# Perceiver block on one core: context columns of two tiles loaded transposed, tail groups of 80 rows, scans spread

## What is computed

```python
energy = jnp.einsum('bcn,bmn->bcm', x1, x2)            # x1: layernormed x (16,64,1024), x2: context (16,1601,1024)
attn = jax.nn.softmax(energy, axis=-1)
attn = attn / (RENORM_EPS + attn.sum(axis=1, keepdims=True))
x_r = jnp.einsum('bcm,bmn->bcn', attn, x1_2)           # x1_2: the same context
t = x1 - (jnp.einsum('oc,bcn->bon', conv_w, x_r) + conv_b[None, :, None])
t_hat = (t - mean) * jax.lax.rsqrt(var + BN_EPS)       # mean and var over batch and width
x_r_out = jax.nn.relu(t_hat * bn_gamma[None, :, None] + bn_beta[None, :, None])
return x1 + x_r_out
```

## Time and profile before

| | |
|---|---|
| median of 3 runs | 1380.77 us (1377.85 to 1381.84) |
| the profiled execution | 1379.24 us, its span 1377.4 us |
| TensorE busy (matmuls) | 1334.1 us, 97% |
| VectorE, ScalarE busy | 878.7 us (64%), 495.1 us (36%) |
| DMA | 356.25 MB, mean 259 GB/s; 379 to 422 GB/s in the first 13 of 40 slices |

### The profile page before, as it was taken

One profiled execution on the slowest core, in us unless ns is written; L12 is line 12 of the kernel. 1 busy time (PEld: TensorE's weight loads), 2 busy tenths in 40 slices (PEclk: granted clock), 3 DMA queues, 4 the chain that ended last, 5 costly groups with the idle time before them and its releaser, 6 DMA issues.

```text
span 1377.4 us, 17833 instructions
## 1 busy us (share of the span) xinstructions
PE 1334.1 (97%) x6850; PEld 651.2 (47%) x6850; DVE 878.7 (64%) x1484; ACT 495.1 (36%) x765; POOL 2.4 (0%) x10
## 2 busy tenths in 40 slices
PE   7999999999999979999999999999999999999994
PEld 4554646444454434444555555444444444444442
DVE  3232424324242288888889996755999997777974
ACT  1121302113021122116877775112545455544432
POOL 0000000000000000000000000000000000000000
PEclk9999999999999989999999999999999999999998
DMA  9999999999999587845565669341487775222264
GB/s 379 419 421 420 421 422 420 422 421 421 417 398 393 234 321 255 315 168 164 161 182 154 172 174 339 107 168 52 167 271 226 242 264 196 77 77 77 77 180 152
DMA packets 141044, 356.25 MB, mean 259 GB/s; under 512 B 63008, under 2 KB 89760, under 8 KB 115360
## 3 DMA queue, kind: packets, MB, share of 16 engines
q1 hardware_dynamic: 137792, 343.56, 68.5%
q10 hardware_dynamic: 3168, 11.54, 2.1%
HBM read 308.40 MB, written 46.66 MB: 258 GB/s over the span
## 4 chain that ended last, share of the span: by engine, by line
PE 74%; issue 14%; DMA 6%; DVE 4%; ACT 1%; DVEq 0%; POOLq 0%; POOL 0%
PE ps L1048 13%; PE ps L1153 13%; PE ps L1309 9%; PE ps L1220 8%; PE ps L962 7%; PE ps L1269 6%; PE ps L1107 5%; PE ps L1000 4%; DMA ctxT<-in_ctxT 3%; PE ps L979 2%; PE ps L1030 2%; PE ps L982 2%; DMA w_scan<-in_w2t 1%; PE ps L1173 1%; DMA x_t<-in_x 1%
## 5 line engine op out<-in xcount | busy, mean ns | idle before, releaser
L1358 PE MATMUL ps<-t_half,hl 128*128 128x512 f16 x896 | 193.6, 379 | 0.0
L1048 PE MATMUL ps<-ctx_sb,attnT 128*64 128x512 f32 (+1 forms) x832 | 180.3, 593 | 0.0
L699 ACT ACTIVATE stg<-ps 128x512 f32<-128x512 f32 (+1 forms) x80 | 44.4, 555 | 345.5 <-PE ps L979 173.4
L1358 PEld LDWEIGHTS ps<-t_half,hl 128*128 128x128 f16 x896 | 87.7, 98 | 105.7
L962 PE MATMUL ps<-ctxT,x1T 128*64 128x512 f32 x512 | 115.8, 596 | 1.8 <-DMA ctxT<-in_ctxT 1.8
L872 ACT ACTIVATE hl<-hb,al 128x512 f16<-128x512 f32 x112 | 79.2, 720 | 97.4 <-PE ps L1358 83.7
L1048 PEld LDWEIGHTS ps<-ctx_sb,attnT 128*64 128x64 f32 (+1 forms) x832 | 58.9, 137 | 115.4 <-issue 108.0
L1862 DVE SCALAR_TENSOR_TENSOR hl<-hb,al,hl 128x512 f16<-128x512 f32 x112 | 81.9, 749 | 48.7 <-ACT hl L872 48.5
L1107 PE MATMUL ps<-wv_sb,x2T 128*128 128x512 f32 x256 | 112.0, 596 | 0.0
L1220 PE MATMUL ps<-wo_sb,oT 128*128 128x512 f32 x256 | 111.6, 593 | 0.3 <-ACT oT L778 0.3
L1456 DVE COPY stg<-ps 128x512 f32<-128x512 f32 (+1 forms) x80 | 50.9, 639 | 82.2 <-PE ps L982 43.0
(11 more groups left out here) (220 smaller groups left out, 1810.5 us busy)
## 6 DMA issues: line engine op xcount, KB each, us to landing
ctxT<-in_ctxT SPq DMA_DIRECT2D x64, 1024.0 KB, 22.4
ctx_sb<-in_ctx SPq DMA_DIRECT2D x40, 1024.0 KB, 17.3
ctx_sb<-in_ctx SPq DMA_DIRECT2D x8, 4096.0 KB, 28.3
ctx_sb<-in_ctx SPq DMA_DIRECT2D x16, 2048.0 KB, 32.5
w_scan<-in_w1t SPq DMA_DIRECT2D x32, 512.0 KB, 6.4
w_buf<-in_w1t SPq DMA_DIRECT2D x32, 512.0 KB, 4.1
w_scan<-in_w2t SPq DMA_DIRECT2D x32, 512.0 KB, 5.5
w_buf<-in_w2t SPq DMA_DIRECT2D x32, 512.0 KB, 4.7
```

The costliest lines, as they stand in the source:

```text
L1048: ins = mm(bank(ea + hf)[C * b:C * b + C, :], attnT[0:w, slots[mt], C * b:C * b + C], ctx_sb[0:w, mt, b, hf * BANK:hf * BANK + BANK], star ...
L1358: ins = mm(bank(b), hl[:, r % RING, n, s * P:s * P + P], t_half[:, r % BRING, :], start=(fresh and k == 0 and n == 0), stop=(k == HK - 1 a ...
```

## The change

It has five parts.

1. For tile 6 the wide columns (positions 1024 to 1535) of all eight 128s of the width come transposed from memory: `in_ctxW`, four loads of 1 MiB through the ring `ctxT` behind the tile's eight chunks. TensorE multiplies them directly (`loaded_energies`), and only the two tail pairs are transposed.
2. For tile 7 the wide columns come so too, two loads through the ring and two "apart" into `stg`, and the tail columns as `in_ctxE`, two loads of 0.25 MiB into `tails`. The apart and tail loads have one semaphore, and TensorE waits for all four ahead of the third wide load. Tile 7 has no transposes of context at all.
3. The row group of block 12 is loaded as 80 rows (0.625 MiB) for 128, in all eight tiles.
4. SP's order for tiles 6 and 7 is another (below), and `tok` and `xo` are loaded as two row tiles each at first and the rest behind `wv_sb`.
5. VectorE's first part has 40 scans for 48, placed before, within and behind the row tiles' work (`V_SCANS`); the second part has 24 for 16, four per row tile.

With this `make_x1` of tile 7 is called behind the copy of the first tail pair and the maximum over the chunk energies, and the relu of row tile 2 behind ScalarE's copies for row tile 0.

```diff
@@ -41,6 +41,7 @@
+TAIL_ROWS = TAIL + (-TAIL) % 16
...
@@ -56,16 +57,40 @@
-PAIRS = [("wide", c) for c in range(NC)] + SINGLES[-2:]
-E = len(PAIRS)
-assert len(SINGLES) == E
+LOADED = (0,) * (NT - 2) + (8, NC)
+def pairs(p):
+    if p < BY_ROW:
+        return SINGLES
+    return [("wide", c) for c in range(LOADED[p], NC)] + (SINGLES[-2:] if p < NT - 1 else [])
+def first_pair(p):
+    return sum(len(pairs(q)) for q in range(p))
+def slots_of_tile(p):
+    ring = [(p, "chunk", c) for c in range(NC)] + [(p, "wide", i) for i in range(LOADED[p] // 2 if p < NT - 1 else 2)]
+    return ring if p < NT - 1 else ring + [(p, "apart", i) for i in range(2)]
+USES = [use for p in range(NT) for use in slots_of_tile(p)]
+USE_NO = {use: n for n, use in enumerate(USES)}
+RING_NO = {use: n for n, use in enumerate([use for use in USES if use[1] != "apart"])}
+RING_USES = list(RING_NO)
-SCANS_V = 48
+SCANS_V = 40
+V_SCANS = (0, 0, 2, 6, 7, 7, 7, 7, 4)
...
@@ -143,6 +168,7 @@
+        tails = [sb("tail0", [P, NC // 2, 2, TAIL], 168 * KB), sb("tail1", [P, NC // 2, 2, TAIL], 180 * KB)]
...
@@ -405,15 +443,28 @@
             sp.dma_start(x_t[:, :], x_v[0]).then_inc(x_in, 16)
             sp.dma_start(cst[:, :], consts).then_inc(cst_in, 16)
-            def load_T(q, chunks):
+            def load_T(q, chunks, kind="chunk"):
                 for c in chunks:
-                    k = NC * q + c
+                    use = (q, kind, c)
+                    k = RING_NO[use]
                     if k >= SLOTS:
-                        sp.wait_ge(ctxT_used, k - SLOTS + 1)
-                    sp.dma_start(ctxT[:, k % SLOTS, :, :], ctxT_in[q, c]).then_inc(ctxT_got[k % SLOTS], 16)
+                        sp.wait_ge(ctxT_used, USE_NO[RING_USES[k - SLOTS]] + 1)
+                    to, src = (slot(use), ctxT_in[q, c]) if kind == "chunk" else (halves(use), ctxW_in[q, c])
+                    sp.dma_start(to, src).then_inc(ctxT_got[k % SLOTS], 16)
+
+            def load_apart():
+
+                sp.wait_ge(e_done, first_pair(NT - 1))
+                for i in range(2):
+                    sp.dma_start(slot((NT - 1, "apart", i)), ctxW_in[NT - 1, 2 + i]).then_inc(apart_got, 16)
+                for i in range(2):
+                    sp.dma_start(tails[i][:, :, :, :], ctxE_in[i]).then_inc(apart_got, 16)
             def load_N(q, g):
                 m0, m1 = N_GROUPS[g][0], N_GROUPS[g][-1] + 1
+                if m1 == MT:
+                    sp.dma_start(ctx_sb[0:TAIL_ROWS, m0, :, :], ctx[q, m0 * P:m0 * P + TAIL_ROWS]).then_inc(ctx_in[g], 16)
+                    return
                 sp.dma_start(ctx_sb[:, m0:m1, :, :], ctx[q, m0 * P:m1 * P].rearrange("(t p) b n -> p t b n", p=P))\
                   .then_inc(ctx_in[g], 16)
...
@@ -445,28 +496,49 @@
                     next_N(range(1, 5))
                 else:
                     load_T(p + 1, range(7, NC))
+                    load_T(p + 1, range(min(LOADED[p + 1] // 2, 2)), "wide")
+                    if p + 1 == NT - 2:
+                        next_N((4, 0))
+                        load_T(p + 1, range(2, 4), "wide")
+                        next_N((1,))
+                        load_T(p + 2, range(0, 2))
+                        next_N((2, 3))
+                        load_T(p + 2, range(2, 4))
+                        next_N(range(5, G))
+                        load_T(p + 2, range(4, 6))
+                        continue
+                    if p + 1 == NT - 1:
+                        load_apart()
+                        next_N((5, 7, 0, 1, 2, 6, 3, 4))
+                        break
                     next_N(range(0, 5))
                 if p == 0:
                     sp.dma_start(lam_sb[:, 0:4 * D], lambdas.partition_broadcast(P)).then_inc(lam_in, 16)
                 if p + 2 < NT:
-                    load_T(p + 2, range(0, 4 if p < 2 else 2))
+                    load_T(p + 2, range(0, 4 if p < 2 or LOADED[p + 1] else 2))
                 next_N(range(5, 6))
-                if p >= 2 and p + 2 < NT:
+                if p >= 2 and p + 2 < NT and not LOADED[p + 1]:
                     load_T(p + 2, range(2, 4))
                 next_N(range(6, G))
                 if p + 2 < NT:
                     load_T(p + 2, range(4, 6))
-            sp.wait_ge(ctxT_used, NC * NT)
+            def load_tok(t0, t1):
+                sp.dma_start(tok[:, t0:t1, :], n_dram[t0:t1].rearrange("t p n -> p t n")).then_inc(n_in, 16)
+
+            def load_xo(t0, t1, s):
+                sp.dma_start(xo[:, t0:t1, :], x_v[t0:t1].rearrange("t p n -> p t n")).then_inc(s, 16)
+
+            sp.wait_ge(ctxT_used, len(USES))
             sp.wait_ge(n_stored, 16 * (NT - 1))
-            sp.dma_start(tok[:, 0:NT - 1, :], n_dram[0:NT - 1].rearrange("t p n -> p t n")).then_inc(n_in, 16)
+            load_tok(0, 2)
             sp.wait_ge(pv_done, G * NT - 7)
-            for i in range(2):
-                h4 = slice(4 * i, 4 * i + 4)
-                sp.dma_start(xo[:, h4, :], x_v[h4].rearrange("t p n -> p t n")).then_inc(s_in[i], 16)
+            load_xo(0, 2, s_in[0])
             sp.wait_ge(pv_done, G * NT - 3)
             sp.dma_start(wv_sb[:, :, :], wv.rearrange("(c p) n -> p c n", p=P)).then_inc(wv_in, 16)
+            load_tok(2, NT - 1)
+            load_xo(2, NT, s_in[1])
             sp.wait_ge(pv_done, G * NT)
             def scan_load(n, buf):
...
@@ -739,6 +811,9 @@
+                if t == 0:
+                    act.wait_ge(n_in, 32)
+                    relu(2)
...
@@ -1001,17 +1076,41 @@
+            def loaded_energies(p):
+                wides = [u for u in slots_of_tile(p) if u[1] != "chunk"]
+                for j, use in enumerate(wides):
+                    if use[1] == "apart":
+                        pe.wait_ge(apart_got, 64)
+                    else:
+                        k = RING_NO[use]
+                        pe.wait_ge(ctxT_got[k % SLOTS], 16 * (k // SLOTS) + 16)
+                    for i in range(2):
+                        c = 2 * j + i
+                        for b in range(2):
+                            ins = mm(bank(2)[C * b:C * b + C, :], x1T[:, p % 2, c, C * b:C * b + C], halves(use)[:, i, b, :],
+                                     start=(c == 0), stop=(c == NC - 1))
+                    ins.then_inc(ctxT_used, 1)
+            def tail_energies(p):
+                for c in range(NC):
+                    for b in range(2):
+                        ins = mm(bank(3, TAIL)[C * b:C * b + C, :], x1T[:, p % 2, c, C * b:C * b + C],
+                                 tails[c // 4][:, c % 4, b, :], start=(c == 0), stop=(c == NC - 1))
+                ins.then_inc(e_done, 1)
-                for e in range(4, E, 2):
+                n = len(pairs(p))
+                for e in range(4, n, 2):
-                two(pair_energies, p, E - 2)
+                two(pair_energies, p, n - 2)
...
@@ -1073,7 +1172,16 @@
-                if p + 1 < NT:
+                if p + 1 < NT and LOADED[p + 1]:
+                    chunk_energies(p + 1, range(4, NC))
+                    if p == 5:
+                        loaded_energies(6)
+                        two(pair_transposes, 6, 0)
+                        later_pairs(6)
+                    else:
+                        loaded_energies(7)
+                        tail_energies(7)
+                elif p + 1 < NT:
...
@@ -1435,8 +1543,8 @@
-                if t % 4 == 0:
-                    V.wait_ge(s_in[t // 4], 16)
+                if t in (0, 2):
+                    V.wait_ge(s_in[t // 2], 16)
@@ -1450,20 +1558,25 @@
-                    if E * p + e >= 4:
-                        V.wait_ge(e_done, E * p + e - 3)
+                    if first_pair(p) + e >= 4:
+                        V.wait_ge(e_done, first_pair(p) + e - 3)
-                    if e == 7:
-                        V.wait_ge(ctxT_used, NC * (p + 1))
+                    if e == max(len(pairs(p)) - 3, 0):
+                        V.wait_ge(ctxT_used, used_by(p))
-                    if e == 5 and p + 1 < NT:
+                    if e == max(len(pairs(p)) - 5, 0) and p + 1 < NT:
-                V.wait_ge(e_done, E * p + E - 2)
+                if p < NT - 1:
+                    V.wait_ge(e_done, first_pair(p + 1) - 2)
+                else:
+                    V.wait_ge(ctxT_used, used_by(p))
+                    own.done(V.tensor_reduce(mx4[:, 0:1], ps[:, ea * BANK:(ea + 2) * BANK], AX.X, ALU.max))
+                    V.wait_ge(ctxT_used, len(USES))
-                V.wait_ge(e_done, E * p + E)
+                V.wait_ge(e_done, first_pair(p + 1) if p < NT - 1 else first_pair(p) + 1)
...
@@ -1528,11 +1643,20 @@
-            def norm2(t):
+            def next_scans(n):
+                for _ in range(n):
+                    scan(scanned_tiles[0], w_scan)
+                    scanned_tiles[0] += 1
+                    if scanned_tiles[0] == WT:
+                        V.wait_ge(scanned, WT)
```

(48 more changed lines are left out.)

25 lines of the change are left out of this document (13 added, 12 removed).

## The result

| | before | changed |
|---|---|---|
| median | 1379.77 us (4 runs, 1377.85 to 1381.84) | 1396.21 us (4 runs, 1394.23 to 1399.87) |
| profiled execution, its span | 1379.24, 1377.4 us | 1399.87, 1398.1 us |
| TensorE busy | 1334.1 us | 1328.5 us |

The ratio is 1.0126 with a 95% interval of 1.0105 to 1.0146: slower by 16.4 us by the medians, 18.4 over the forecast. The profiled execution is the slowest of the four, so its trace shows 20.7 us more span than the one before, where the medians are 16.4 apart. The page first: TensorE's busy share, the granted clock, the DMA engines' share and what they moved, in 40 slices.

What follows compares the result with a forecast made beforehand. TensorE and DMA were taken to be at their limit together: of 16.4 us taken from TensorE, late loads leave 2.2. That gives 1377.0 us from the profiled run, 1378.6 from the median; forecast 1377.8, range 1373 to 1384.

Steps and rivals of the forecast that it cites:

- I take the whole group's 2.49 us, the nearest row there is: Tail group loads, all eight tiles: an 80-row load takes as long as the 128-row group, 2.49 us.
- rival 4: Tail loads: the 80 rows spread badly, sixteen on each of five engines, 4.98 us a load; 1390 us, chance 0.12.
- to spare: Context attention, per tile: 22 MiB take the DMA 54.8 us beside TensorE's 57.96 us, leaving 3.2 us.
- DMA dry from: Tile 6's third and fourth wide loads wait for chunks: DMA dry from about 369, issue at 374.0, first byte 376.9.
- TensorE waits for x1: Behind tile 6's tail pairs: VectorE makes the next tile's x1 late, TensorE waits 387.4 to about 390.5, 3 us.
- apart loads land, TensorE's wait: Tile 7: apart and tail loads land at 442.9, after TensorE has waited 4.4 us from 438.5.
- aggregation, first value product: Behind the last tile: xo lands at 480.2, aggregation at 484.2, value products from 494.6; gain 2.2 us out of 16.4.
- clock loss behind the wait: TensorE after its wait for tile 7's apart loads: a lower granted clock costs some 1.5 us.
- spare time of row tile 2 with spread scans: Row tile 2's operand is ready at 515.2, TensorE wants it at 516.9: 1.7 us to spare, scans cost nothing.
- Rival 1: Tail loads: 80 rows cost what their bytes cost, 1.56 us; gain 5.1 us, 1374.9 us, chance 0.30.
- Rival 2: Tiles 6 and 7: the queue keeps up and TensorE sets the pace; 11.9 us won, 1368 us, chance 0.06.
- Rival 3: Scans, the x1 wait or slower 4 KB rows of tok and xo eat the gain; 1.3 us lost, 1381, chance 0.10.

Runs made afterwards that it cites:

- experiment 1: The changed kernel with its tail groups loaded as 128 rows again, nothing else different: 1377.09 us, ratio to before 0.9981.
- experiment 5: Loads alone, no kernel: one 80-row load for a 128-row one among full loads cost 0.5 us more with engines in step, 2.7 to 3.0 out of step.
- experiment 6: Changed kernel with 128-row tail groups, three row groups of tile 6 moved ahead of its third wide load: 1371.17 us, 0.9929; three further variants 1369.00 to 1371.30 us.
- experiment 3: Scans placed as before in the changed kernel with 128-row tail groups: 1390.98 us; new scan placement alone in the kernel before: 1378.60 us.

## Why the prediction was wrong

The failed step is "I take the whole group's 2.49 us, the nearest row there is" for the 80-row load. It is the one term of the sum that was far off: in this kernel such a load costs its 2.49 us and 2.0 to 4.6 us more, in the full loads around it too. The right rival was 4, by sign and kind, with the wrong mechanism (sixteen rows on five engines), too small a price (2.49 us more each, for 3.5 on average) and too few loads: it counts those up to the wait at 229 and one in the last stream, but two more lie between (tiles 4 and 5) and added 8.5 us. What the prediction missed is that a shape that costs nearly nothing on its own can slow its neighbours, and that the 16 engines were out of step in the kernel before already: 2.7 us apart in tile 1's loads, 5.8 in tile 5's.

How the loads' cost becomes TensorE's can be read off load by load, since SP issues its loads in the same order in both kernels up to tile 6's last chunk. "Engines apart" is the distance between the 16 arrivals of a full load just ahead of the tile's tail group, in the changed kernel; "stream later" is how much later than before a load behind that group lands, and "added" the part of it that this tile brought; the last column is how much later TensorE ends the weighing of the tile.

| tile | engines apart | stream later | added | weighing ends later |
|---|---|---|---|---|
| 0 | 2.6 us | 2.0 us | 2.0 | 2.1 us |
| 1 | 3.3 | 4.7 | 2.7 | 2.0 |
| 2 | 3.9 | 8.2 | 3.5 | 3.2 |
| 3 | 5.5 | 12.6 | 4.4 | 14.7 |
| 4 | 6.1 | 16.5 | 3.9 | 14.7 |
| 5 | 7.8 | 21.1 | 4.6 | 19.3 |

With full tail groups (experiment 1) the same six loads land within 0.9 us of the kernel before. The price grows along with the distance between the engines, except from tile 3 to 4; that the distance is the reason rests on experiment 5. The 3.2 us a tile that the DMA has "to spare" by the prediction don't soften it at first: at 226 to 229 the kernel before has no lead, TensorE waits there for chunks too (0.5 us twice). So the 12.6 us come through whole, 3.2 by which TensorE is late already and the wait of 8.75, and behind the wait it runs at a granted clock of 0.50 until 244.6, which by the 5.8 us worked at it is 2.9 us more, an estimate. A wait of 3.04 us for a row group at 337.1, with 3.2 us at the same clock behind it, makes the last 4.6. A chunk load takes a median of 27.6 us from issue to landing in 288 to 346, for 20.2 before. The 80-row loads of tiles 6 and 7 take what was to be won behind: from the end of tile 5's weighing to the first value product it is 125.8 us, and 122.5 in experiment 1. Taken out of the changed kernel the loads give back 19.0 us by the medians, and put alone into the kernel before they cost 20.7.

The other steps, read from experiment 1, where the failed one is taken out:

| step | predicted | measured |
|---|---|---|
| DMA dry from; third wide load of tile 6 lands | 369; 379.4 (first byte 376.9) | 368.4; 378.0 (first byte 374.4) |
| TensorE waits for x1 | 3 us | 3.05 |
| waits for chunks 2, 3 of tile 7 | 2 | 1.21 |
| apart loads land, TensorE's wait | 442.9, 4.4 us | 441.7, 4.39 |
| weighing of tile 7 starts | 457.0 | 455.65 |
| xo lands | 480.2 | 479.3 |
| aggregation, first value product | 484.2, 494.6 | 483.1, 493.65 |
| clock loss behind the wait | 1.5 us | 1.5 in the changed kernel (4.79 us for 3.17), none here (3.14) |
| spare time of row tile 2 with spread scans | 1.7 us | 1.9 (514.2 to 516.08) |
| time | 1377.8 us | 1377.09 us |

So the rest of the mechanism was right. That the stream's places fit within 1 to 2 us has a little luck in it: it starts 2.5 us earlier than predicted, and the apart loads, 26.5 MiB later, land only 1.2 us earlier.

Rival 1 (bytes) is out: no stream of fewer rows paid by bytes. Rival 2 is out for the kernel as given, and half true of experiment 6, where filling the gap won 6.7 us (9.3 against 2.6 under the runs of before). Rival 3 is out: spread scans hold nothing up (experiments 1 and 3), and x1 made early wins nothing.
